# The last layer of a graph kernel: another order of the messages' additions, joined operations in the coefficient chain, eight buffers of tails

## What is computed

```python
ricci = _l2_normalize(tail_emb + rel_emb)
hyper_head = expmap0(head_emb)
hyper_tail = expmap(tail_emb, hyper_head)
hyper_rel = expmap(rel_emb, hyper_head)
res = project(mobius_add(hyper_tail, hyper_rel))
res = logmap(res, hyper_head) + ricci * 1e-07
res = jax.nn.relu(res)
sums = jnp.zeros((n_entities, res.shape[-1]), res.dtype).at[head].add(res)
```

## Time and profile before

| | us |
|---|---|
| median of three unprofiled runs (5222.07 to 5224.58) | 5223.61 |
| span of the profiled execution | 6351.7 |
| VectorE busy in it | 3726.5 (59%) |
| GpSimd busy in it | 3463.1 (55%) |
| TensorE busy in it | 2842.1 (45%) |
| ScalarE busy in it | 1728.7 (27%) |
| last layer's first gather | at 3205.9 |
| a full step of the last layer, profiled | 116.6 to 123.5 |

### The profile page before, as it was taken

One profiled execution on the slowest core, in us unless ns is written; L12 is line 12 of the kernel. 1 busy time (PEld: TensorE's weight loads), 2 busy tenths in 40 slices (PEclk: granted clock), 3 DMA queues, 4 the chain that ended last, 5 costly groups with the idle time before them and its releaser, 6 DMA issues. The chain is left out here.

```text
span 6351.7 us, 75027 instructions
## 1 busy us (share of the span) xinstructions
PE 2842.1 (45%) x17919; PEld 2271.2 (36%) x17920; DVE 3726.5 (59%) x6870; ACT 1728.7 (27%) x5084; POOL 3463.1 (55%) x3375
## 2 busy tenths in 40 slices
PE   4544588433343334477614434434431343444442
PEld 1333456223333333345403333333331233333332
DVE  6444544255555666444426776667673767667678
ACT  0255200011111111000003354344340335445434
POOL 5667445466555663544265565566525556556551
PEclk7655699666666666678855555555555555555555
DMA  3720400355555554400021111111102111111110
GB/s 101 171 94 1 127 1 1 105 154 172 167 171 169 173 173 143 139 4 1 8 49 42 37 42 37 37 41 38 33 10 50 40 37 42 37 39 41 41 30 13
DMA packets 470914, 446.71 MB, mean 70 GB/s; under 512 B 113322, under 2 KB 417773, under 8 KB 470268
## 3 DMA queue, kind: packets, MB, share of 16 engines
q1 hardware_dynamic: 230602, 227.94, 12.4%
q0 software_dynamic: 116768, 136.51, 9.0%
q10 hardware_dynamic: 123282, 79.08, 4.5%
HBM read 306.93 MB, written 136.34 MB: 70 GB/s over the span
## 5 line engine op out<-in xcount | busy, mean ns | idle before, releaser
L2412 POOL DMA_INDIRECT tg<-tab_d,tail_ids x1632 | 1711.2, 1049 | 1191.1 <-DVEq L2731 644.9
L458 POOL DMA_INDIRECT sorted_edges_d<-place_batch x784 | 825.0, 1052 | 657.1 <-issue 220.6
L2437 PE MATMUL hr<-near_table,near_hot 128*128 x4896 | 654.4, 278 | 926.2 <-issue 593.1
L1598 POOL DMA_INDIRECT xg<-tab_d,src_i x784 | 768.0, 980 | 501.1 <-issue 241.6
L2445 PE MATMUL acc<-msg,sum_hot 128*96 128x65 f32 x3264 | 559.8, 364 | 902.1 <-ACT msg L2519 701.3
L2437 PEld LDWEIGHTS hr<-near_table,near_hot 128*128 128x128 f16 x4896 | 505.6, 108 | 1075.7 <-issue 970.2
L2445 PEld LDWEIGHTS acc<-msg,sum_hot 128*96 128x96 f32 x3264 | 536.4, 277 | 924.8 <-issue 924.7
L2492 ACT ACTIVATE pr<-hr 128x396 f32<-128x396 f32 x576 | 272.2, 482 | 1235.0 <-DMA b2col<-in_L_gnn_be_dram 786.9
L2513 ACT ACTIVATE pr<-pr,coef_c 128x64 f32<-128x64 f32 x1496 | 380.7, 340 | 82.4 <-issue 79.4
L2506 ACT ACTIVATE msg<-tg,coef_b 128x64 f32<-128x64 f32 x1632 | 399.1, 340 | 2.6 <-DVEq L2926 2.6
L2743 DVE TENSOR_REDUCE scal<-prod 128x17 f32<-128x1088 f32 x288 | 370.5, 1286 | 9.8
(11 more groups left out here) (504 smaller groups left out, 5392.9 us busy)
## 6 DMA issues: line engine op xcount, KB each, us to landing
ex<-spread_d SPq DMA_DIRECT2D x112, 448.0 KB
msg_d<-back ACTq DMA_DIRECT2D x112, 448.0 KB
near_hot<-head_row_d SPq DMA_DIRECT2D x96, 408.0 KB
tg<-tab_d,tail_ids POOLq DMA_INDIRECT x1632
spread_d<-zeros ACTq DMA_DIRECT2D x28, 896.0 KB
spread_d<-zeros SPq DMA_DIRECT2D x28, 896.0 KB
idsU<-dst_short_d SPq DMA_DIRECT2D x112, 224.0 KB
pairs_d<-pair_m SPq DMA_DIRECT2D x3, 4800.0 KB
```

The lines of the kernel that those rows point to most:

```text
L458: l.eng.indirect_dma_start(K.sorted_edges[:, :], bass.IndirectOffsetOnAxis(ap=K.batch[:, n % 2, 0, k:k + 1], axis=0), K.batch[:, n % 2, 1, ...
L1598: l.eng.indirect_dma_start(xg[j.c % ROWS][:, half * H + k, :], None, K.tab1, bass.IndirectOffsetOnAxis(ap=src_i[:, t:t + 1], axis=0)).then ...
L2412: e.indirect_dma_start(tg[:, u % TAILS * GQ + k, :], None, K.tab3, bass.IndirectOffsetOnAxis(ap=K.tail_ids[:, u * GQ + k:u * GQ + k + 1], ...
L2437: ins = e.matmul(hr[(u * FILLS + g) % 2][:, c:c + PW3], near_hot[u % HOTS][:, k, :], rows[:, bass.ds(at[k] + n * PW3, PW3)], start=n == 0, ...
```

## The change

- The two additions of a quarter stand apart. gather_up is cut into sum_keys (the comparison), add_heads (product and first addition) and add_kinds (second addition), and takes all four quarters. For p and p+1 the comparison of p+1 stands between the additions of p, and near(n) between those of p+1; for p+2 and p+3 each quarter's own comparison stands between its additions.
- In the chain neighbouring columns of scal are handled by one operation of 136, 204 or 272 elements where two to four of 68 or 136 stood. For that q2 and n2 swap places, kB and kC become one tile, A, B and C are used as one block abc, and PP is copied into scal beside P.T and P.R (heads).
- The tails' and kinds' lengths are fetched with two strided copies and PP with one, where ten copies stood.
- TAILS is 8, so that the tails of a step lie in one block T_; prod is one tile of two halves.

The core of the diff:

```diff
-TAILS = 9
+TAILS = 8
...
+        def gather_up(p, n, mark):
+            sum_keys(p)
+            add_heads(p)
+            sum_keys(p + 1)
+            add_kinds(p)
+            mark()
+            add_heads(p + 1)
+            if n is not None:
+                near(n)
+            add_kinds(p + 1)
+            mark()
+            if n is not None:
+                near(n + 1)
+            for u in (p + 2, p + 3):
+                add_heads(u)
+                sum_keys(u)
+                add_kinds(u)
+                mark()
...
-            tt0(x[0], B, pt, MUL)
-            tt0(x[1], C, pr, MUL)
-            tt0(x[2], A, PP_, MUL)
+            tt0(terms[:, 0:3, :], abc, heads, MUL)
             tt0(x[3], C, tr, MUL)
-            tt0(x[4], B, q2[:, 0, :], MUL)
-            tt_(x[5], C, C, MUL)
+            tt_(terms[:, 4:6, :], abc[:, 1:3, :], q2, MUL)
...
-            v.tensor_copy(q2[:, 1, :], R_[:, :, D])
-            for q in range(QN):
-                at = slice(q * GQ, (q + 1) * GQ)
-                v.tensor_copy(q2[:, 0, at], tg[:, tails(now + q), D])
-                v.tensor_copy(n2[:, 0, at], tg[:, tails(now + q), D + 1])
-            v.tensor_copy(n2[:, 1, :], R_[:, :, D + 1])
+            both_of = lambda x: x.rearrange("p k c -> p c k")
+            v.tensor_copy(sc[:, 2:25:22, :], both_of(T_[:, :, D:D + 2]))
+            v.tensor_copy(sc[:, 3:26:22, :], both_of(R_[:, :, D:D + 2]))
+            v.tensor_copy(PP, PP_)
...
-            tt_(X2, u2, both(PP_), MUL)
+            tt_(X2, u2, both(PP), MUL)
...
-            tt0(a2, a2, u2, MUL)
-            tt_(b2, b2, u2, MUL)
+            ab2 = sc[:, 10:14, :].rearrange("p (n two) m -> p n two m", two=2)
+            tt_(ab2, ab2, u2.unsqueeze(1).to_broadcast([P, 2, 2, M]), MUL)
...
-            tt0(A1(16), b2[:, 1, :], PR, MUL)
-            tt0(A1(17), a2[:, 1, :], PT, MUL)
-            tt_(A1(18), b2[:, 1, :], TR, MUL)
+            tt0(A2(16), both(b2[:, 1, :]), A2(dPR), MUL)
+            tt_(A1(18), a2[:, 1, :], PT, MUL)
...
-            tt0(A1(16), A1(16), u2[:, 1, :], ADD)
-            tt_(A1(17), A1(17), A1(18), ADD)
+            tt_(A2(16), A2(16), sc[:, 9:19:9, :], ADD)
...
-            tt0(A1(16), A1(16), a2[:, 0, :], MUL)
-            tt0(A1(17), A1(17), b2[:, 0, :], MUL)
+            tt0(A2(16), A2(16), sc[:, 10:13:2, :], MUL)
...
-            tt0(A1(6), A1(6), A1(18), MUL)
-            tt_(A1(7), A1(7), A1(18), MUL)
-            l.eng.wait_ge(l.sem, l.done())
-            tt0(A1(16), A1(6), a2[:, 0, :], MUL)
-            tt0(A1(17), A1(7), a2[:, 1, :], MUL)
-            tt0(cB, A1(6), b2[:, 0, :], MUL)
-            tt_(cC, A1(7), b2[:, 1, :], MUL)
+            tt_(A2(6), A2(6), both(A1(18)), MUL)
+            l.eng.wait_ge(l.sem, l.done())
+            tt_(sc[:, 25:29, :].rearrange("p (n two) m -> p n two m", two=2), A2(6).unsqueeze(1).to_broadcast([P, 2, 2, M]), ab2, MUL)
...
-            for c in (cA, cB, cC):
-                tt_(c, c, f, MUL)
+            tt0(abc, abc, three(f), MUL)
...
-            tt0(A1(16), cA, PP_, MUL)
-            tt0(A1(17), cB, PT, MUL)
-            tt_(A1(18), cC, PR, MUL)
+            tt_(sc[:, 16:19, :], abc, heads, MUL)
...
-            for c in (cA, cB, cC):
-                tt_(c, c, A1(17), MUL)
+            tt_(abc, abc, three(A1(17)), MUL)
...
-            tt0(cB, cB, om, MUL)
-            tt_(cC, cC, om, MUL)
+            tt_(A2(27), A2(27), both(om), MUL)
             l.eng.wait_ge(l.sem, l.done())
-            tt0(kB[s][:, :], cB, g, ADD)
-            tt_(kC[s][:, :], cC, g, ADD)
+            tt_(coef_bc[s][:, :, :], A2(27), both(g), ADD)
```

More of the change, by code:

```diff
@@ L2343, in edge_loop3 @@
     tg = sb("tg3", [P, TAILS * GQ, RW], F32)
-    prod = two("prod3", [P, GQ, D], F32)
+    prod = sb("prod3", [P, 2 * GQ, D], F32)
     msg = [sb(f"msg3{q}", [P, GQ, D + 1], F32) for q in range(QN)]
@@ L2347, in edge_loop3 @@
     cA, cB, cC = (sc[:, n, :] for n in (26, 27, 28))
-    kB, kC = (two(n, [P, M], F32) for n in ("coef_b", "coef_c"))
-    terms = prod[0][:, :, :].rearrange("p k f -> p (k f)")[:, 0:9 * M].rearrange("p (n m) -> p n m", m=M)
+    coef_bc = two("coef_bc", [P, 2, M], F32)
+    kB, kC = ([c[:, n, :] for c in coef_bc] for n in range(2))
+    terms = prod[:, :, :].rearrange("p k f -> p (k f)")[:, 0:9 * M].rearrange("p (n m) -> p n m", m=M)
     zero = pr[1][:, 0:2, :].rearrange("p k f -> p (k f)")[:, 0:256].bitcast(F16)
@@ L2731, in mark, with dot @@
                 v.sem_inc(paced, 1)
-            def dot(n, x, y, quarters, taken=False, landed=False):
-                for q in quarters:
+            def dot(n, x, y, halves, taken=False, landed=False):
+                for q in range(2 * halves.start, 2 * halves.stop):
+                    at, cells = slice(q * GQ, (q + 1) * GQ), prod[:, q % 2 * GQ:(q % 2 + 1) * GQ, :]
                     u = now + q
@@ L2746, in dot @@
                 v.wait_ge(l.sem, l.done())
-            head = lambda q: P_[:, q * GQ:(q + 1) * GQ, 0:D]
-            kind = lambda q: R_[:, q * GQ:(q + 1) * GQ, 0:D]
-            tail = lambda q: tg[:, tails(now + q), 0:D]
+            T_ = tg[:, s * M:(s + 1) * M, :]
             def ask_scalar(k):
@@ L2756, in ask_scalar @@
                 v.wait_ge(answered, j * NA + k)
-            dot(dPR, head, kind, range(QN), taken=True)
-            dot(dPT, head, tail, range(2), landed=True)
-            dot(dTR, tail, kind, range(2))
-            for q in range(QN):
-                if not first:
-                    gather_up(p + q)
-                mark()
-                if not last and q == 1:
-                    near(n)
-                    near(n + 1)
-            dot(dPT, head, tail, range(2, QN), landed=True)
-            dot(dTR, tail, kind, range(2, QN))
+            dot(dPR, P_, R_, range(2), taken=True)
+            dot(dPT, P_, T_, range(1), landed=True)
+            dot(dTR, T_, R_, range(1))
+            if not first:
+                gather_up(p, None if last else n, mark)
+            else:
+                near(n)
+                near(n + 1)
+                v.sem_inc(paced, QN)
+            dot(dPT, P_, T_, range(1, 2), landed=True)
+            dot(dTR, T_, R_, range(1, 2))
             PT, PR, TR, d2 = A1(dPT), A1(dPR), A1(dTR), A2(dPT)
-            q2, n2, s2, t2, u2, a2, b2, X2 = A2(24), A2(2), A2(4), A2(6), A2(8), A2(10), A2(12), A2(14)
+            PP, heads, abc = A1(dPT - 1), sc[:, dPT - 1:dPT + 2, :], sc[:, 26:29, :]
+            q2, n2, s2, t2, u2, a2, b2, X2 = A2(2), A2(24), A2(4), A2(6), A2(8), A2(10), A2(12), A2(14)
             ask = A2(0)
             om = A1(23)
-            v.tensor_copy(q2[:, 1, :], R_[:, :, D])
-            for q in range(QN):
-                at = slice(q * GQ, (q + 1) * GQ)
-                v.tensor_copy(q2[:, 0, at], tg[:, tails(now + q), D])
-                v.tensor_copy(n2[:, 0, at], tg[:, tails(now + q), D + 1])
-            v.tensor_copy(n2[:, 1, :], R_[:, :, D + 1])
+            both_of = lambda x: x.rearrange("p k c -> p c k")
+            v.tensor_copy(sc[:, 2:25:22, :], both_of(T_[:, :, D:D + 2]))
+            v.tensor_copy(sc[:, 3:26:22, :], both_of(R_[:, :, D:D + 2]))
+            v.tensor_copy(PP, PP_)
             ts_(om, PP_, -1.0, 1.0, MUL, ADD)
@@ L2862, in vector @@
             ask_scalar(2)
-            v.reciprocal(A2(18), ask).then_inc(l.sem, l.add(1))
+            v.reciprocal(X2, ask).then_inc(l.sem, l.add(1))
             l.eng.wait_ge(l.sem, l.done())
-            f, g = A1(18), A1(19)
+            f, g = A1(14), A1(15)
+            three = lambda x: x.unsqueeze(1).to_broadcast([P, 3, M])
             ts0(f, f, 1.0 - 0.004, 1.0, MUL, MIN)
@@ L2900, in vector @@
             l.eng.wait_ge(l.sem, l.done())
-            form(A1(0), cA, cB, cC, PP_, PT, PR, TR, q2)
+            form(A1(0), abc, heads, TR, q2)
             ts0(A1(0), A1(0), 1e-30, None, MAX)
@@ L2927, in vector @@
             mark()
-        for u in range(QUARTERS - QN, QUARTERS):
-            gather_up(u)
+        gather_up(QUARTERS - QN, None, lambda: None)
         v.wait_ge(added, QUARTERS)
```

31 lines of the change are left out of this document (18 added, 13 removed).

## The result

The changed kernel takes 5240.5 us against 5225.3 us for the kernel before on the same chip (medians of 10 runs each), ratio 1.0027 with a 95% interval of 1.0018 to 1.0037. It is slower by 15 us where I forecast 40 us less; the time lies outside my range. A second comparison, on another chip, gives 5234.7 against 5220.2, again 1.0027 (1.0017 to 1.0036).

What follows compares the result with a forecast made beforehand. VectorE (90.5 us a clean step) and GpSimd's gather queue (92.0) were taken as level. VectorE's sum of 55 us, capped by GpSimd at 30, was taken as 40: 5223.6 - 40 = 5183 us, 8-in-10 range 5140 to 5231.

Steps and rivals of the forecast that it cites:

- Clean step: Full step of the last layer without late signals: 90.5 us, with VectorE nearly always busy.
- Chain and copies together: VectorE's coefficient operations joined, 1.96 us saved a step, plus three copies for ten, 0.35 us.
- Part of the additions: Four quarters' comparisons, products and additions on VectorE: end moves from 25.67 to 24.54 us, a gain of 1.13.
- the new wait at the first answer: VectorE waits 1.3 us for ScalarE's first answer, since TensorE runs 1.58 us later.
- GpSimd's cap: Gather queue of 92.0 us a step becomes 90.9 by less contention; if it sets the pace, 30 us in all.
- case 2: GpSimd sets the pace and isn't relieved; only 5 us behind the last gather gained: 5218; chance 0.16.
- case 1: VectorE saves and GpSimd gives part back: between 30 and 55 us, taken 40: 5183; chance 0.58.
- theory J: Experiments' theory: joined operations or the order lengthen gathers wherever they stand; delaying the product gives no gain, 5234 to 5240.
- The relay of the additions: In the additions, reordering swaps VectorE's wait for TensorE for a shorter one for ScalarE; gain 1.13 us.
- Case 3: Later rectification costs 1.6 us a step at the question, joining saves little: 5235; chance 0.13.
- Case 4: Late signals also occur unprofiled and work slips into them: between 47 and 100 us, taken 65: 5159; chance 0.13.
- Eight buffers: Gathers wait for tails of u-8 to be scaled; a cover of 6.8 us hides it, priced at nothing.

Runs made afterwards that it cites:

- chain alone: Changed kernel with the old order of gather_up put back (joined operations, copies, eight buffers stay); 5227.1 us against 5220.7 for the kernel before, ratio 1.0014.
- order alone: Kernel before with only the new order of additions in gather_up; 5224.5 us against 5220.7 for the kernel before, ratio 1.0004.

## Why the prediction was wrong, point by point

**VectorE's terms were right.** Clean step: 90.5 predicted, 91.0 measured. Chain and copies together: 1.96 + 0.35 = 2.31 predicted, 2.17 measured; 696 instructions less. The copies alone went from 0.93 to 0.52 us, 0.41 less. The prediction's second price for the two new copies (0.31 each) is not borne out by the trace with the chain alone: the next operation follows them after 0.20 and 0.19. Part of the additions: 25.67 to 24.54 predicted, 25.75 to 24.56 measured. The first rectification was forecast 7.4 us behind the first comparison, and TensorE's two additions from there. The timeline of the step above (ScalarE, then TensorE):

```profile
3165.95 1.11 ACT L2520 ACTIVATE msg<-msg 128x1088 f32<-128x1088 f32 x1 [4.84 <-DVE msg L2594]
```

```profile
3167.30 5.70 PE L2446 MATMUL acc<-msg,sum_hot 128*96 128x65 f32 x34 [26.89 <-ACT msg L2520]
3174.23 5.70 PE L2446 MATMUL acc<-msg,sum_hot 128*96 128x65 f32 x34 [1.24 <-issue]
```

That is 7.45, 8.80 and 15.73 us behind 3158.50. The wait for the kinds of p+2 is 0.75 (0.86), the new wait at the first answer 1.11 with the order alone (1.3). In the whole change that last wait doesn't appear, since VectorE comes later, after its wait for tails. The joined operations behaved as priced, one of 204 followed after 0.29 us, while one of 272 was followed by a dependent one after 0.47, not 0.36:

```profile
3125.39 0.37 DVE L2562 TENSOR_TENSOR scal<-scal 128x204 f32<-128x204 f32 x1
3125.68 0.22 DVE L2559 TENSOR_TENSOR prod<-scal 128x68 f32<-128x68 f32 x1
```

```profile
3113.11 0.44 DVE L2559 TENSOR_TENSOR scal<-scal 128x272 f32<-128x272 f32 x1
3113.58 0.30 DVE L2562 TENSOR_TENSOR scal<-scal 128x136 f32<-128x136 f32 x1
```

**The step that failed is GpSimd's cap, in three places.**

First, its size. The 92.0 us a step that I worked out from the mean gather (the terms as written give 91.7) were near the truth (68 x 1.342 = 91.3 by the quiet page). I then took a pitch between that mean and 1.30, with the reason that the order removes contention. The row was better than my choice, and case 2, GpSimd setting the pace, was nearer than case 1.

Second, the relief of 0.38 in three of four quarters. I took each operation beside a gather as 0.20 us. The rows show otherwise; with the order alone, VectorE and GpSimd:

```profile
3239.12 1.29 DVE L2558 TENSOR_TENSOR msg<-msg,pr 128x1088 f32<-128x1088 f32 x1
3240.32 1.85 DVE L2574 TENSOR_TENSOR sum_hot<-head_keys,beside 128x1632 f32<-128x1632 f32 x1
```

```profile
3239.47 1.75 POOL L2412 DMA_INDIRECT tg<-tab_d,tail_ids  x1 [0.30 <-issue]
```

The gather starts 0.35 behind the addition and ends 2.10 behind it: one addition is enough to make a gather of 1.75. Gathers of 1.70 to 1.80 did not become rare, as I forecast: 28 before, 47 with the order alone, 49 in after. In the table below the additions with their comparisons and scalings cost 83.7 us before and 75.5 with the order alone, 77.8 and 78.0 in the two traces of the change. Over the 22 steps that have them that is 0.3 to 0.4 us a step and not 1.1.

Third, and this turned the sign, I priced the contention of the dot products as fixed. It depends on where in a gather the product starts. Before, the fourth quarter's product started 0.25 or 0.26 us behind the start of a gather in 17 of 20 full steps. After, it starts when the tails land, 0.04 to 1.20 us behind one, 0.8 in the mean. GpSimd's timeline around the product that starts at 3188.70:

```profile
3187.92 0.94 POOL L2413 DMA_INDIRECT tg<-tab_d,tail_ids  x1 [0.30 <-issue]
3189.17 1.64 POOL L2413 DMA_INDIRECT tg<-tab_d,tail_ids  x1 [0.30 <-issue]
3191.11 0.94 POOL L2413 DMA_INDIRECT tg<-tab_d,tail_ids  x1 [0.30 <-issue]
```

The product starts 0.78 us behind the gather of 3187.92, the next one starts 0.47 behind the product and ends at 3190.81, 2.11 behind it. In every quiet trace all gathers that start 0.07 to 1.1 us behind such a product end 2.10 or 2.11 us behind it (18 to 21 rows in each of five traces). So a product that starts x behind a gather lengthens the next one by about x - 0.08, up to x = 1.17. The same holds at two other places, which moved too. The step's first product before:

```profile
3213.63 0.94 POOL L2412 DMA_INDIRECT tg<-tab_d,tail_ids  x1 [0.30 <-issue]
3214.88 0.94 POOL L2412 DMA_INDIRECT tg<-tab_d,tail_ids  x1 [0.30 <-issue]
```

It starts at 3213.65, 0.02 behind a gather, and costs nothing. After, at 3136.86:

```profile
3136.52 0.94 POOL L2413 DMA_INDIRECT tg<-tab_d,tail_ids  x1 [0.30 <-issue]
3137.77 1.20 POOL L2413 DMA_INDIRECT tg<-tab_d,tail_ids  x1 [0.30 <-issue]
```

0.34 behind one, at a cost of 0.26. And the third quarter's product, 0.19 behind a gather before, falls 0.51 behind one with the new order (after, at 3182.98, beside the gather that began at 3182.47 and takes 1.41, since the addition ahead of it holds it too). In the table each gather's time over 0.943 us is charged to the last product, comparison, scaling or addition of VectorE in the same hop begun before the gather's end. Summed over both hops, us:

| gathers' time over 0.943 each, beside | before | order alone | chain alone | change (two traces) |
|---|---|---|---|---|
| first two products of a step | 6.3 | 5.6 | 15.2 | 15.3, 17.3 |
| third quarter's P.T | 5.1 | 10.6 | 5.6 | 12.5, 11.5 |
| fourth quarter's P.T | 6.8 | 6.6 | 11.4 | 13.8, 16.8 |
| additions, comparisons, scaling by A | 83.7 | 75.5 | 83.6 | 77.8, 78.0 |
| all else | 59.3 | 60.2 | 58.8 | 58.7, 59.7 |
| GpSimd busy with gathers (pages) | 1700.2 | 1697.4 | 1713.5 | 1717.2, 1722.2 |

The chain brings the first and third lines, the order the second and the relief of the fourth.

Why the chain moves the first product can be read from the rows too. The last product of a step and the first of the next, in the kernel before, with the order alone and with the chain alone:

```profile
3269.04 1.29 DVE L2558 TENSOR_TENSOR prod<-tg,pr 128x1088 f32<-128x1088 f32 x1
3304.62 1.30 DVE L2558 TENSOR_TENSOR prod<-pr 128x1088 f32<-128x1088 f32 x1 [0.32 <-DVE coef_c L2558]
```

```profile
3268.51 1.29 DVE L2558 TENSOR_TENSOR prod<-tg,pr 128x1088 f32<-128x1088 f32 x1
3305.33 1.31 DVE L2558 TENSOR_TENSOR prod<-pr 128x1088 f32<-128x1088 f32 x1 [0.32 <-DVE coef_c L2558]
```

```profile
3273.07 1.29 DVE L2559 TENSOR_TENSOR prod<-tg,pr 128x1088 f32<-128x1088 f32 x1
3306.50 1.29 DVE L2559 TENSOR_TENSOR prod<-pr 128x1088 f32<-128x1088 f32 x1 [0.32 <-DVE coef_bc L2559]
```

In all 20 full steps of each of the five traces the last product starts 0.23 or 0.24 us behind a gather. From there to the next step's first product it is 35.58 us before and 36.82 with the order alone. That is 1.24 more, one undisturbed gather and the idle time before it (0.94 + 0.30), and the first product falls where it fell, 0.01 to 0.02 behind a gather. With the joined operations it is 33.43, which is 2.15 less and no whole number of gathers, and the product falls 0.34 or 0.35 behind one in most steps.

The queue is 17.0 and 22.0 us longer; the two comparisons are 14.5 and 15.2 us slower. VectorE saves some 2.3 us behind the last gather of each hop, so the last layer grew by less than the queue: by 12.4 and 17.3 us in the two traces. For the chain alone it is 13.3 in the queue and 8.6 in the layer; the 6.4 of the medians (interval 3 to 12) agree. That the phases of these products make up the difference is read from the traces; that a shifted product would take it back was put to runs and not tested on a quiet chip. What the table does speak against is theory J for the joined operations themselves: none of the growth lies beside the chain (it is in "all else", which is level). The Trainium skill (GPSIMD Engine Reference, 8. Key points) says that VectorE's instructions with two SBUF inputs contend with GpSimd for the SBUF interfaces. The traces agree, from 0.94 alone to as much as 2.04 us for a gather beside a product, and add that the price hangs on the moment of the start.

**The relay of the additions was right and worth nothing.** Case 3 lost no time by it: the order alone is even. Its place and size (1.11 us at the first answer) are as worked out, but the chain's saving was never in doubt, so that case was not what made the kernel slower.

**The late signals were misread.** I put them down to the profiled execution because 1128 us were missing from the median. They belong to a kind of chip and stand in unprofiled runs there. Case 4's mechanism is real on those, and its 47 to 100 us too small: 165 to 168 for the order, 56 to 65 for the chain. It had to be left out of the sum for the median shown, which is of a quiet chip; that I did, for a wrong reason.

**Eight buffers.** Priced at nothing. All gathers of after but the first of each hop have only 0.30 or 0.31 us before them, none waits for scaled tails, and the gathers' idle time is 531.7 us with nine and with eight. On a chip with late signals eight alone gave 0.9974; on a quiet one it was not run alone.

**The last step of a hop** was to be 3.4 us shorter. The waits of 1.37 and 1.09 are gone as forecast, and the one for ScalarE ahead of the second addition of p+2 is 1.31 (0.9). I had not seen two others: 0.53 for TensorE at the comparison, and above all 2.65 for tails:

```profile
3910.15 1.85 DVE L2575 TENSOR_TENSOR sum_hot<-head_keys,beside 128x1632 f32<-128x1632 f32 x1 [0.53 <-PE acc L2446]
3913.31 1.29 DVE L2594 TENSOR_TENSOR msg<-msg,pr 128x1088 f32<-128x1088 f32 x1 [1.31 <-ACT pr L2514]
3925.34 1.29 DVE L2559 TENSOR_TENSOR prod<-pr,tg 128x1088 f32<-128x1088 f32 x1 [2.65 <-DMA tg<-tab_d,tail_ids]
```

It lasts 88.5 us against 89.5.

## What to carry to other kernels

When two engines are level, a saving on one is worth no more than the distance to the other, and it must be asked what the handed-over wait does to the engine that now leads: here VectorE saved some 3 us a step and, by starting its products at other moments, cost GpSimd 0.7 to 0.9. Where a mean duration hides an operation that takes 0.94 us or up to 2.0, list its rows by the moment at which the other engine's operation starts, before a saving is priced. And when profile and median differ by a fifth, compare the kernel before with itself on both kinds of run before a cause is named.

## What the runs showed of the hardware

- Same program, same data: 5220 to 5225 us in three comparisons and 6290 to 6298 us in four, on other chips. In the last layer the difference lies in signals between engines, which arrive late while gathers run: 9.7 us behind the end of the work at one comparison of a full step, and at once in a last step, which has almost no gathers. What makes a chip one or the other stays open.
- On a quiet chip VectorE and the gathers keep one phase for many steps: the first product 0.01 to 0.02 us behind a gather in 17 of 20 steps, the next three 0.26, 0.30 and 0.30. Behind the first gather of a hop none waits longer than the 0.30 or 0.31 of issue, so no semaphore times them. Contention keeps the two in step: a caught gather ends 2.11 behind a product, the next starts 0.30 later, and the next product 2.72 behind the first, which is 0.31 behind that gather.
- A gather that starts 0.07 to 1.1 us behind the start of a product with two SBUF operands (1.29 us long) ends 2.10 or 2.11 us behind that start. One that runs already keeps its 0.94.
